# First attention: maxima in four places of 512 columns in place of two of 1024, each maxima matmul behind a score matmul

## The reference

```python
q = (hidden_states @ Wq + bq).reshape(b, s, NH, HD).transpose(0, 2, 1, 3)
k = (hidden_states @ Wk + bk).reshape(b, s, NH, HD).transpose(0, 2, 1, 3)
v = (hidden_states @ Wv + bv).reshape(b, s, NH, HD).transpose(0, 2, 1, 3)
scores = jnp.einsum('bhqd,bhkd->bhqk', q, k) / jnp.sqrt(jnp.asarray(HD, q.dtype))
mod = jax.nn.sigmoid(hidden_states @ cg_W + cg_b + (cons_vec @ am_W + am_b))
scores = scores * mod.transpose(0, 2, 1)[..., None]
probs = jax.nn.softmax(scores, axis=-1)
ctx = jnp.einsum('bhqk,bhkd->bhqd', probs, v).transpose(0, 2, 1, 3).reshape(b, s, h)
```

## Time and profile before

| | us |
|---|---|
| median of 3 runs | 3048.09 |
| lowest, highest | 3040.52, 3054.56 |
| the profiled execution | 3030.39 |
| its span, first to last instruction | 3028.6 |
| first group's maxima alone | 197 to 238 |
| the 16 groups of the first attention | 238 to 1048 |

### The profile page before, as it was taken

One profiled execution on the slowest core, in us unless ns is written; L12 is line 12 of the kernel. 1 busy time (PEld: TensorE's weight loads), 2 busy tenths in 40 slices (PEclk: granted clock), 3 DMA queues, 4 the chain that ended last, 5 costly groups with the idle time before them and its releaser, 6 DMA issues. The chain is left out here.

```text
span 3028.6 us, 42693 instructions
## 1 busy us (share of the span) xinstructions
PE 2765.4 (91%) x14144; PEld 1787.5 (59%) x14145; DVE 2019.9 (67%) x3033; ACT 1424.6 (47%) x2556; POOL 980.7 (32%) x1000
## 2 busy tenths in 40 slices
PE   7989999999999889999998999868998679999995
PEld 6754545555545345555555555446666459888895
DVE  4568777777777298887887888555665557333337
ACT  2315666666666634444443544433444343233334
POOL 4457530000000044343345555453000360343322
PEclk9979999999999999999999999978999899999998
DMA  6999985353533155555555453345665433323425
GB/s 219 316 257 271 243 225 76 49 75 50 78 46 47 28 126 144 156 163 157 146 155 150 127 139 98 103 134 97 114 109 92 128 103 113 134 78 111 174 84 167
DMA packets 246189, 400.00 MB, mean 132 GB/s; under 512 B 37711, under 2 KB 147895, under 8 KB 244727
## 3 DMA queue, kind: packets, MB, share of 16 engines
q1 hardware_dynamic: 177940, 251.20, 31.4%
q10 hardware_dynamic: 49299, 82.70, 12.9%
q0 software_dynamic: 18768, 63.79, 6.7%
HBM read 231.46 MB, written 166.14 MB: 131 GB/s over the span
## 5 line engine op out<-in xcount | busy, mean ns | idle before, releaser
L654 DVE TENSOR_REDUCE an_m<-an_psm 128x1 f32<-128x1024 f32 x512 | 595.4, 1217 | 181.6 <-PE an_psm L578 181.5
L635 ACT ACTIVATE an_probs<-an_pst 128x512 f32<-128x512 f32 x1024 | 539.8, 605 | 304.4 <-PE an_pst L608 299.7
L1409 ACT ACTIVATE wj_probs<-wj_pst 128x512 f32<-128x512 f32 x512 | 297.7, 595 | 347.4 <-PE wj_pst L1251 338.6
L1126 POOL TENSOR_TENSOR wj_sums<-wj_sums,wj_probs 128x512 f32<-128x512 f32 x192 | 267.6, 1394 | 312.7 <-ACT wj_probs L1409 309.6
L1440 DVE TENSOR_REDUCE wj_m<-wj_pm 128x1 f32<-128x512 f32 x512 | 324.0, 679 | 17.4 <-PE wj_pm L1226 16.8
L1240 PE MATMUL wj_pacc<-wj_probs,wj_vs 128*64 128x512 f32 x1024 | 249.4, 608 | 2.8 <-ACT wj_probs L1409 2.8
L578 PE MATMUL an_psm<-an_ks,an_qs 127*128 127x512 f32 x640 | 224.5, 432 | 6.2 <-DVE an_m L654 6.2
L608 PE MATMUL an_pst<-an_qs,an_ks 128*128 128x512 f32 x640 | 209.7, 404 | 8.1 <-ACT an_probs L635 7.0
L1166 POOL MEMSET wj_qs<- 64x2048 f32 x2 | 3.5, 1800 | 620.1 <-issue 620.1
L1251 PE MATMUL wj_pst<-wj_qs,wj_ks 128*128 128x512 f32 x512 | 203.7, 398 | 0.0
L1126 DVE TENSOR_TENSOR wj_sums<-wj_sums,wj_probs 128x512 f32<-128x512 f32 x192 | 179.4, 935 | 20.2 <-ACT wj_probs L1409 20.2
(11 more groups left out here) (431 smaller groups left out, 6009.4 us busy)
## 6 DMA issues: line engine op xcount, KB each, us to landing
ew_w<-scr_ws SPq DMA_DIRECT2D x10, 3072.0 KB, 12.0
scr_ws<-wide_pair POOLq DMA_DIRECT2D x27, 1024.0 KB, 5.6
ac_qs<-scr_xq ACTq DMA_DIRECT2D x48, 256.0 KB, 5.1
an_qs<-scr_q SPq DMA_DIRECT2D x40, 256.0 KB, 11.6
an_ks<-scr_k SPq DMA_DIRECT2D x40, 256.0 KB, 13.1
wj_qs<-scr_mq ACTq DMA_DIRECT2D x18, 512.0 KB, 5.1
wj_ks<-scr_mk ACTq DMA_DIRECT2D x18, 512.0 KB, 5.9
scr_xs<-x_acc SPq DMA_DIRECT2D x2, 4128.0 KB, 15.9
```

Source lines behind the costliest of these rows:

```text
L635: act.activation(probs[:, (NSTEP * G + s) % HELD, j], pst[:, (GH * s + j) % RING], ACT.Exp, scale=HD ** -0.5).then_inc(exp_done, 1)
L654: dve.tensor_reduce(m1[:, hq, col:col + 1], psm[:, n % 2], AX.XY, ALU.max).then_inc(mx_done, 1)
L1126: eng.tensor_tensor(sums[:, x % CPB, j], earlier, probs[:, s % RING, j], ALU.add).then_inc(sum_done[j], 1)
L1409: act.activation(probs[:, x % RING, j], pst[:, j], ACT.Exp, scale=BHD ** -0.5).then_inc(exp_done, 1)
```

## The change

`psm` is four places of one bank each (`MB = 4`). Each maxima matmul takes a place by itself, waits for the reduction four matmuls back, and increments `mx_ready`. VectorE reduces 512 columns at a time into two columns of `m1`, and `finish` has one more instruction, a maximum of the two (L660 of the new numbering). In a step each of the four score matmuls is followed by one maxima matmul, and the value products stand behind the third maxima matmul of an even step, where they stood ahead of a pair. Value products were issued for two steps at once already.

```diff
+        MB = 4
...
-        m1 = k.sb("m1", [P, CPB, GH * NT])
+        m1 = k.sb("m1", [P, CPB, 2, GH * NT])
...
-        psm = k.ps("psm", [P, 2, 2, CH])
+        psm = k.ps("psm", [P, MB, CH])
...
-                if kh == 0:
-
-                    pe.wait_ge(mx_done, NM * G + n + 1)
+                part = 2 * (NM * G + n) + kh
+                if part >= MB:
+
+                    pe.wait_ge(mx_done, part - MB + 1)
                 q0 = (hq * NT + i) * P
-                last = pe.matmul(psm[:, n % 2, kh], qs[slot][0:MROW, j, q0:q0 + P], ks[slot][0:MROW, j, kh * CH:(kh + 1) * CH],
-                                 start=True, stop=True)
-                if kh == 1:
-                    last.then_inc(mx_ready, 1)
+                pe.matmul(psm[:, part % MB], qs[slot][0:MROW, j, q0:q0 + P], ks[slot][0:MROW, j, kh * CH:(kh + 1) * CH],
+                          start=True, stop=True).then_inc(mx_ready, 1)
...
+                        if G + 1 < B * NG:
+                            maxima(*nxt, 2 * s + j // 2, j % 2)
                         if x and x % 2 == 0 and j == 2:
                             values(x - 2)
                             values(x - 1)
-                        if G + 1 < B * NG and j % 2 == 0:
-                            for kh in range(2):
-                                maxima(*nxt, 2 * s + j // 2, kh)
...
-                    dve.wait_ge(mx_ready, NM * G + n + 1)
                     col = j * NT + i
-                    dve.tensor_reduce(m1[:, hq, col:col + 1], psm[:, n % 2], AX.XY, ALU.max).then_inc(mx_done, 1)
+                    for kh in range(2):
+                        part = 2 * (NM * G + n) + kh
+                        dve.wait_ge(mx_ready, part + 1)
+                        dve.tensor_reduce(m1[:, hq, kh, col:col + 1], psm[:, part % MB], AX.X, ALU.max).then_inc(mx_done, 1)
...
-                dve.wait_ge(mx_done, 2 + NM * G + (hq + 1) * NM // CPB)
-                dve.tensor_scalar(mneg[:, 0:GH * NT], m1[:, hq], -1.0, None, ALU.mult).then_inc(m_chain, 1)
-                dve.wait_ge(m_chain, 2 * (CPB * G + hq) + 1)
+                dve.wait_ge(mx_done, 2 * (NM * G + (hq + 1) * NM // CPB))
+                dve.tensor_tensor(m1[:, hq, 0], m1[:, hq, 0], m1[:, hq, 1], ALU.max).then_inc(m_chain, 1)
+                dve.wait_ge(m_chain, 3 * (CPB * G + hq) + 1)
+                dve.tensor_scalar(mneg[:, 0:GH * NT], m1[:, hq, 0], -1.0, None, ALU.mult).then_inc(m_chain, 1)
...
-            dve.sem_inc(mx_done, 2)
```

More of the change, by code:

```diff
@@ L651, in maxima @@
                     hq, j, i = mx_list[n]
-                    dve.wait_ge(mx_ready, NM * G + n + 1)
                     col = j * NT + i
-                    dve.tensor_reduce(m1[:, hq, col:col + 1], psm[:, n % 2], AX.XY, ALU.max).then_inc(mx_done, 1)
+                    for kh in range(2):
+                        part = 2 * (NM * G + n) + kh
+                        dve.wait_ge(mx_ready, part + 1)
+                        dve.tensor_reduce(m1[:, hq, kh, col:col + 1], psm[:, part % MB], AX.X, ALU.max).then_inc(mx_done, 1)
             def finish(G, hq, first):
-                dve.wait_ge(mx_done, 2 + NM * G + (hq + 1) * NM // CPB)
-                dve.tensor_scalar(mneg[:, 0:GH * NT], m1[:, hq], -1.0, None, ALU.mult).then_inc(m_chain, 1)
-                dve.wait_ge(m_chain, 2 * (CPB * G + hq) + 1)
+                dve.wait_ge(mx_done, 2 * (NM * G + (hq + 1) * NM // CPB))
+                dve.tensor_tensor(m1[:, hq, 0], m1[:, hq, 0], m1[:, hq, 1], ALU.max).then_inc(m_chain, 1)
+                dve.wait_ge(m_chain, 3 * (CPB * G + hq) + 1)
+                dve.tensor_scalar(mneg[:, 0:GH * NT], m1[:, hq, 0], -1.0, None, ALU.mult).then_inc(m_chain, 1)
+                dve.wait_ge(m_chain, 3 * (CPB * G + hq) + 2)
                 dve.transpose(mturn[:], mneg[:]).then_inc(m_chain, 1)
-                dve.wait_ge(m_chain, 2 * (CPB * G + hq) + 2)
+                dve.wait_ge(m_chain, 3 * (CPB * G + hq) + 3)
                 if not first:
```

## The result

The changed kernel takes 3002.47 us (median of 4 runs, 2998.17 to 3005.39) against 3048.04 us for the kernel before: a ratio of 0.985, 95% interval 0.9824 to 0.9876. That is 45.6 us less. The prediction was 3003 us.

What follows compares the result with a forecast made beforehand. TensorE was taken as the bound, waiting for VectorE's reductions in the burst behind value products. TensorE -45.6, start-up -1.8 and transfers +2.5 sum to -44.9 us, from 3048.1 to 3003 us, range 2990 to 3028.

Steps and rivals of the forecast that it cites:

- Part 1, TensorE: Attention groups with maxima beside them: no maxima matmul waits in a plain period, 6.17 to 5.79 us; -45.6 us in all.
- long periods: Two of a group's eight periods, at the first score matmul and the copy-out, counted as gaining the same 0.38 us.
- backlog of three: Burst behind value products: eight maxima written, VectorE clears five, and the three left fit in four places.
- Part 2, VectorE: Reductions of 512 columns at 0.60 us each; VectorE's group takes 40.8 us, under TensorE's 46.3, so hidden.
- Rival 1: VectorE's reductions do not overlap, 0.68 us each; a group gains 2.2 us, total 3020 us; chance 0.12.
- Part 3, start-up: Maxima before the first group, VectorE setting the pace: 40.6 us becomes 38.4 plus 0.4 for added maxima, -1.8 us.
- the small steps of `finish`: VectorE's steps at each half group's end: hidden by TensorE, showing some 0.3 us twice a group where they meet a burst.
- Part 4, transfers: Rows of maxima sent out and back before 420 us come late in shorter groups: 2.5 us given back, between 0 and 9.
- signs of being wrong: Reductions at 0.68 us or more, score weight loads waiting several times a period, or late rows at several group ends before 420 us.
- Rival 2: No gain: in the burst the scores' ring stops TensorE, opening about four score weight loads a period; 3048 us; chance 0.08.
- Rival 3: VectorE becomes the bound at 0.77 us a reduction, slower from 0.76; groups 51.7 us, total 3068 us; chance 0.04.

Runs made afterwards that it cites:

- the memsets: Changed kernel with a memset of 16, 128 or 256 columns on VectorE ahead of each reduction: 3007.23, 3022.51 and 3099.29 us.
- The paced kernels: GpSimd's weight splitting spread over the attention: changed kernel 2993.06 us, with the score ring also counted on over groups 2976.53, kernel before 3039.66.
- the later set on one chip: Changed kernel unaltered, run again beside three kernels with GpSimd's splitting spread out: 3003.31 us against 3046.89 for the kernel before, ratio 0.986.
- the run with 0.819: Changed kernel with a memset of 256 columns on VectorE ahead of each reduction, 0.819 us a reduction: 3099.29 us against 3042.39 for the kernel before.

## Why the prediction was right

**Part 1, TensorE.** 5.79 us a period was predicted and is measured. A group has three long periods and not two, and they were said to gain 0.38 us each; they gain 0.22 (the middle of a group, where weight loads of the scores wait for ScalarE, which has a copy-out there), 0.32 (group start) and 0.56 (copy-out), 1.10 in place of 1.14 together. A group is 2.95 us shorter (50.95 to 48.00), 3.04 were forecast. No maxima matmul of a plain period waits, and the run with three places shows that the fourth place is needed for it, as the backlog of three had said. The Trainium skill (TensorE: Matmul & The Clock Gate, The cost: per-tile semaphore tail) would have had four more increments a period cost 0.10 us. The trace shows none: with an increment at each matmul the distance stays 0.23 us. These are not concurrent tiles, for which the section gives its figure.

**Part 2, VectorE.** Reductions come each 0.60 us, as in the second attention. Rival 1, that they would not overlap, is out. The sentence of the Trainium skill (VectorE: DVE Perf Modes, The DRAIN you can't avoid) that the prediction took for it, that the next operation doesn't start before the pipeline is empty, is only half of what the section says: it adds that a next operation that is not held starts earlier. The rows agree with the addition: the next reduction starts 0.08 us before the one ahead of it ends, though there is a wait between them. The gain I gave the rival was a little high: at 0.68 us a group was to gain 2.2 us, and at 0.686, reached with the memsets, it gained 1.7.

**Part 3, start-up.** Right about its rate and wrong about its end. The first value products come at 244.85 us, 0.5 later than before (244.36), where 1.8 less were forecast; counted from the first maxima matmul it is 1.0 us more (48.35 against 47.37). VectorE's timeline, GpSimd's and TensorE's:

```profile
217.40 19.22 DVE L655 TENSOR_REDUCE an_m<-an_psm 128x1 f32<-128x512 f32 x32
236.66 1.96 DVE L660 TENSOR_TENSOR an_m<-an_m 128x16 f32<-128x16 f32 x1
...
236.21 2.37 POOL L554 TENSOR_TENSOR wide_pair<-an_wraw,wide_pair 128x1024 fp32r<-128x1024 f32 x1
...
237.78 0.39 PE L608 MATMUL an_pst<-first_q,first_k 128*128 128x512 f32 x1
239.94 0.50 PE L580 MATMUL an_psm<-an_ks,an_qs 127*128 127x512 f32 x1 [1.76 <-DVE an_m L655]
...
244.85 0.64 PE L592 MATMUL an_pacc<-an_probs,first_v 128*32 128x512 f32 x4
```

The 32 reductions take 19.22 us, 0.60 each, and the first score matmul is issued at 234.88 us, 2.8 us earlier than before (237.65). But the maximum that `finish` now has, priced at 0.2 us, takes 1.96 us at 236.66: it ends when GpSimd's subtraction does (236.21 + 2.37 = 238.58). The reductions queued behind it wait, and the maxima matmul at 239.94 stands 1.76 us for them. It is not the added instruction as such. In the second profile of the changed kernel the maximum takes 0.47 us and the cast, which was there before, takes the 1.96:

```profile
237.77 1.96 DVE L668 CAST an_mrows<-an_mturn 128x32 fp32r<-128x32 f32 x1
...
237.33 2.36 POOL L554 TENSOR_TENSOR wide_pair<-an_wraw,wide_pair 128x1024 fp32r<-128x1024 f32 x1
```

In the kernel before `finish` came 2.5 us later and met nothing, by 0.03 us:

```profile
236.74 2.38 POOL L553 TENSOR_TENSOR wide_pair<-an_wraw,wide_pair 128x1024 fp32r<-128x1024 f32 x1
...
239.15 0.18 DVE L659 TENSOR_SCALAR an_mneg<-an_m 128x16 f32<-128x16 f32 x1
```

So the step that failed is that the small steps of `finish` were priced as if they ran alone, when the change moves them in time against GpSimd's work. The paced kernels, where GpSimd isn't at work there, show the term as forecast: from the first maxima matmul to the first value products 45.65 and 45.66 us with the change and 47.39 without, -1.7 us.

**Part 4, transfers.** 2.5 us were to be given back, between 0 and 9. The first four groups took 207.5 us before and 197.5 in the first profile after, where 4 x 2.95 = 11.8 were to be gained: 1.8 given back. In the second profile of the changed kernel they took 205.2 us: 9.5 given back, 5.92 of it in one wait (391.62). So the term is right in kind, and its size is a matter of the execution. One of the prediction's own signs of being wrong did show: rows were late at three of the group ends before 420 us, by 2.49, 0.64 and 1.19 us. Their price had been put in, so the total held.

**The sum.** That the medians differ by 45.6 us where 44.9 were forecast is in part luck. The attention of the profiled execution is 41.4 us shorter: 42.0 in the groups, where 43.1 were forecast, and 0.5 lost at the start, where 1.8 were to be gained. In the second profile it is 34.4 us shorter. The rest of the difference of the medians lies in the spread between executions, 7 us over the four runs of the changed kernel and 14 over those of before. In the later set on one chip the medians differ by 43.6 us.

**The rivals.** Rival 2, the scores' ring, would have shown weight loads of the scores waiting for exponentials several times a period; in the plain periods of the groups with maxima beside them, from 420 to 1000 us, there is no such wait. Rival 3 needed 0.76 us a reduction and had 0.60; the run with 0.819 shows that its formula holds once VectorE is the bound.

## What to carry to other kernels

Two buffers of a double unit and four of a single one hold the same data, but the producer waits for a whole unit: where a burst overruns the consumer, count the backlog in units at the burst's end and give it one place more than that (here a backlog of three, where three places waited and four did not; one case). Half-sized instructions are cheap only if the engine overlaps them, so take their cost from the distance of starts and not from their duration. When a stage gets shorter, look for what does not shrink with it: here a chain of small transfers behind bulk ones, which took back up to 10 us and was no longer late when the bulk was paced.

## What the hardware showed that was not expected

A small VectorE instruction can be held by GpSimd for as long as GpSimd's instruction lasts. In the first attention `finish`'s steps take 174 to 214 ns. In the profile of after six of them are longer (1960, 1991, 804, 782, 306 and 277 ns), in that of before six (2250, 1364, 981, 940, 355 and 304 ns). Each ran while GpSimd had a copy, a subtraction or the issue of a transfer under way, and those of over 700 ns ended within 0.1 us of GpSimd's copy or subtraction. The transpose was never among them, nor a reduction from PSUM (674 to 693 ns throughout). Over all fourteen profiles, negations and casts that met GpSimd issuing a transfer took up to 0.50 us, and maxima that met one took 174 to 177 ns. The Trainium skill (SBUF — State Buffer, Who interferes with whom) names the port pair that VectorE shares with GpSimd: a VectorE instruction with two SBUF inputs contends with a GpSimd instruction that reads SBUF, a copy, cast or tensor_scalar can when it uses both ports, and tensor_reduce doesn't. The rows agree, and the added maximum, which has two SBUF inputs, is of the first kind. In the paced kernels no step is longer than 0.5 us.

A memset that runs between reductions costs less than it lasts: 0.072 us long it added 0.013 us a reduction, 0.165 us long 0.088, and 0.272 us long 0.221.
